# The value product of two attention layers, made by tiles of 128 tokens and brought to the layout by pixel by transfers within SBUF

## What is computed

```python
qkv = (x @ W_qkv).reshape(B, N, P, 3, H, hd)
q = qkv[..., 0, :, :].mean(axis=2).transpose(0, 2, 1, 3)
k = qkv[..., 1, :, :].mean(axis=2).transpose(0, 2, 1, 3)
v = qkv[..., 2, :, :].transpose(0, 3, 1, 4, 2).reshape(B, H, N, hd * P)
scores = jnp.einsum('bhnd,bhmd->bhnm', q, k) * hd ** (-0.5)
attn = jax.nn.softmax(scores, axis=-1)
out = jnp.einsum('bhnm,bhme->bhne', attn, v)
out = out.reshape(B, H, N, hd, P).transpose(0, 2, 4, 1, 3).reshape(B, N, P, C)
return out @ W_proj + b_proj
...
x = x + _L0_conv_ref(_ln_c(x), ...)
t = t + _L0_ffn_ref(_ln_t(t), ...)      # 8 experts, the best 2 for each token
```

## Time and profile before

| | |
|---|---|
| Runs | 572.95, 572.11, 576.06 us |
| Profiled execution | 571.98 us, span 570.2 us |
| TensorE (PE) busy | 528.8 us, 93% of the span |
| ScalarE (ACT) busy | 346.2 us, 61% |
| VectorE (DVE) busy | 339.1 us, 59% |
| GpSimd (POOL) busy | 254.0 us, 45% |
| Mean granted clock of TensorE | 0.98 of full speed |
| Value products L1342 | 5.2% of the chain that ended last |

### The profile page before, as it was taken

The page is one execution under the profiler, slowest core; times in us unless marked ns, Lnnn a source line. Parts: engine busy times, 40 slices in busy tenths (PEclk is TensorE's granted clock), DMA queues, the critical chain, the costliest instruction groups (busy, mean ns, idle before and its releaser), DMA issues.

```text
span 570.2 us, 15336 instructions
## 1 busy us (share of the span) xinstructions
PE 528.8 (93%) x3521; PEld 469.5 (82%) x3522; DVE 339.1 (59%) x791; ACT 346.2 (61%) x676; POOL 254.0 (45%) x278
## 2 busy tenths in 40 slices
PE   8899968999999999999879999699999999999992
PEld 4887537989999999999768875399999999999981
DVE  5548974455533555554794578745667676767441
ACT  4778525666645666666457755555777576766530
POOL 4638222444544454453435360424444445645422
PEclk9999979999999999999989999899999999999997
DMA  8436745786432454125442238364365555312110
GB/s 270 150 111 166 255 128 158 241 214 155 114 74 42 145 119 93 35 37 156 136 151 71 84 103 272 117 219 92 88 190 133 138 142 155 59 30 46 32 19 10
DMA packets 49037, 70.54 MB, mean 124 GB/s; under 512 B 9182, under 2 KB 40560, under 8 KB 49008
## 3 DMA queue, kind: packets, MB, share of 16 engines
q1 hardware_dynamic: 35216, 56.41, 31.4%
q0 software_dynamic: 10464, 13.58, 13.3%
q10 hardware_dynamic: 3328, 0.20, 0.4%
HBM read 57.55 MB, written 13.47 MB: 125 GB/s over the span
## 4 chain that ended last, share of the span: by engine, by line
PE 69%; DVE 10%; DMA 7%; ACT 5%; issue 5%; DVEq 2%; ACTq 1%; POOL 1%; POOLq 0%; SPq 0%
PE banks L1301 16%; PE banks L1303 15%; PE banks L1302 15%; PE banks L1514 6%; PE banks L1342 5%; PE banks L1416 2%; DVE stats L907 2%; PE banks L1479 2%; DMA expert_io<-xn_dram,gcol 2%; DMA out_dram<-region_b,scol 1%; DMA mid_dram<-region_b,scol 1%; PE banks L1353 1%; PE banks L1309 1%; ACT region_a L702 1%; ACT onehot_blk L803 1%
## 5 line engine op out<-in xcount | busy, mean ns | idle before, releaser
L1301 PE MATMUL banks<-w_hi,xT_hi 128*128 x336 | 119.4, 355 | 4.0 <-DVE xT_lo L1173 2.6
L1303 PE MATMUL banks<-w_hi,xT_lo 128*128 x336 | 115.0, 342 | 0.0
L1302 PE MATMUL banks<-w_lo,xT_hi 128*128 x336 | 114.2, 340 | 0.0
L1301 PE MATMUL banks<-w_hi,hT_hi 128*128 x364 | 107.9, 296 | 3.9 <-DVE hT_lo L1248 3.9
L1303 PE MATMUL banks<-w_hi,hT_lo 128*128 x364 | 102.8, 283 | 0.0
L1302 PE MATMUL banks<-w_lo,hT_hi 128*128 x364 | 102.8, 282 | 0.0
L638 POOL DMA_INDIRECT mid_dram<-region_b,scol x26 | 49.5, 1905 | 76.4 <-DMA mid_dram<-region_b,scol 28.4
L611 POOL TENSOR_TENSOR w_lo<-raw,w_hi 128x1024 fp32r<-128x1024 f32 (+2 forms) x24 | 58.9, 2471 | 53.2 <-ACT w_hi L686 43.5
L827 ACT COPY banks<-seed_rows 128x672 f32 (+1 forms) x84 | 69.0, 822 | 20.5 <-DVE h_sb L1265 10.7
L638 POOL DMA_INDIRECT out_dram<-region_b,scol x26 | 45.7, 1759 | 71.3 <-DMA expert_io<-xn_dram,gcol 20.3
L1301 PEld LDWEIGHTS banks<-w_hi,hT_hi 128*128 128x128 f32 x364 | 69.3, 190 | 7.0 <-issue 6.3
(11 more groups left out here) (206 smaller groups left out, 899.2 us busy)
## 6 DMA issues: line engine op xcount, KB each, us to landing
raw<-in_L_ffn_w_dram SPq DMA_DIRECT2D x32, 512.0 KB, 3.7
raw<-in_L_ffn_W_dram SPq DMA_DIRECT2D x16, 672.0 KB, 4.1
seed_rows<-in_L_ffn_b_dram SPq DMA_DIRECT2D x8, 672.0 KB, 4.2
seed_rows<-in_L_ffn_b_dram SPq DMA_DIRECT2D x8, 512.0 KB, 4.0
xn_dram<-raw SPq DMA_DIRECT2D x6, 512.0 KB, 3.1
raw<-in_L_ffn_W_dram SPq DMA_DIRECT2D x8, 384.0 KB, 4.1
raw<-in_L_ffn_W_dram SPq DMA_DIRECT2D x8, 256.0 KB
wqkv<-in_L_conv_W_qkv_dram SPq DMA_DIRECT2D x2, 768.0 KB, 5.7
```

Source lines behind the costliest of these rows:

```text
L1301: pe.matmul(out, hi, w_high, start=first, stop=False, skip_group_check=onto)
L1302: pe.matmul(out, hi, w_low, start=False, stop=False, skip_group_check=onto)
L1303: return pe.matmul(out, lo, w_high, start=False, stop=last, skip_group_check=onto)
```

## The change

**Values by tiles.** `values` now makes one of 12 products of 128 tokens by 264 columns per layer, from consecutive columns of `xnT`, into the bank that `V_BANKS[L]` names. ScalarE copies each into one of three free places (`v_parts`: tiles 0 to 4 in `region_d`, 5 to 9 in the third slot of `w_lo`, 10 and 11 in `region_a`). SP then copies the 256 channels of each tile within SBUF, 128 partitions x 1 KB to 8 partitions x 16 KB of `v_sb` (`values_by_pixel`), and the attention product waits for all of them (`v_early`, `v_late`).

**Logits.** They now come out by token. Three small VectorE products `x_part_of` take them from the copies; the way through DRAM is gone, with its two transfers, `v_logits` and L1048.

**Order.** Products, copies and casts are put in another order, in each layer its own. In layer 1 the column sums stand ahead of layer 0's last expert rows, the centring at the start of VectorE's layer 1, tiles 0 and 1 of the values between the transposes, and ScalarE copies the first two transposes and normalises tile 4 before the last deviations. New waits: GpSimd's piece 8 for `x_part_of(1)`; ScalarE's first attention copy for the first five transfers; ScalarE's cast behind the attention copies for all; SP's load of experts 1 and 2 in layer 0, and of expert 2 in layer 1, stand behind transfers in its list.

```diff
...
+V_BANKS = ((6, 7, 4) * 4, (5, 6, 5, 6, 2, 3, 6, 7, 4, 6, 7, 4))
+V_EARLY = 5
...
+        v_parts = [(slice(0, V_EARLY), region_d[:, 0:V_EARLY * (C + E)]),
+                   (slice(V_EARLY, 2 * V_EARLY), w_lo[:, SLOTS - 1, 0:V_EARLY * (C + E)].bitcast(F32)),
+                   (slice(2 * V_EARLY, TILES), region_a[:, TILES * C:TILES * C + (TILES - 2 * V_EARLY) * (C + E)])]
...
+            def values_by_pixel(L, first, end):
+                for i in range(first, end):
+                    sp.wait_ge(lay[L].v, i + 1)
+                    sp.dma_start(v_sb[NPT * i:NPT * (i + 1), :, :], v_tile(i)[:, 0:C]
+                                 ).then_inc(v_early if i < V_EARLY else v_late, 16)
...
+                    if L == 1 and e == 2:
+                        sp.wait_ge(rows_mm, 6)
+                    if e >= 1:
+                        values_by_pixel(L, *((0, V_EARLY, TILES), (0, 0, TILES))[L][e - 1:e + 1])
...
+                    if q == PIECES * (SLOTS - 1):
+                        pool.wait_ge(x_early, 3 * L + 2)
...
-                deviations(0, 0)
-                normalise(0)
-                deviations(1, 0)
-                deviations(2, 0)
-                normalise(1)
...
-                def values_out(j):
-                    if L == 1 and j == 0:
-                        act.wait_ge(lay[0].store, 96)
-                    for q in (2 * j, 2 * j + 1):
-                        act.wait_ge(s.v_mm, q + 1)
-                        nc.scalar.copy(v_sb[:, q, :], bank[V_BANKS[q % 3]][0:BN, 0:C + E]).then_inc(s.v, 1)
+                def values_out(*tiles):
+                    for i in tiles:
+                        act.wait_ge(s.v_mm, i + 1)
+                        nc.scalar.copy(v_tile(i), bank[V_BANKS[L][i]][:, 0:C + E]).then_inc(s.v, 1)
...
+                deviations(0, 0)
+                normalise(range(0, 4))
+                deviations(1, 0)
+                if L == 0:
+                    deviations(2, 0)
+                    normalise(range(4, 8))
+                    transposed(0)
+                    transposed(1)
+                else:
+                    transposed(0)
+                    transposed(1)
+                    normalise(range(4, 5))
+                    deviations(2, 0)
+                    normalise(range(5, 8))
+                    values_out(0, 1)
+                for j in range(2, 6):
+                    transposed(j)
...
+                    if g == 0:
+                        act.wait_ge(x_early, 3 * L + 1)
+                        act.wait_ge(v_early, 16 * V_EARLY * (L + 1))
...
-                values_out(0)
-                first_high(*((1, 2), (4, 5))[L])
-                values_out(1)
-                first_high(*((2, 3), (5, 6))[L])
-                values_out(2)
-                first_high(*((3, 4), (6, 7))[L])
+                    values_out(0, 1)
+                    first_high(1, 2)
+                    values_out(2, 3, 4)
+                    first_high(2, 4)
+                else:
+                    values_out(2, 3)
+                    first_high(4, 5)
+                    values_out(4, 5)
+                    first_high(5, 6)
+                    values_out(6, 7)
+                    first_high(6, 7)
...
                 exponentials(1)
-                values_out(3)
-                first_high(*((4, 5), (7, 8))[L])
+                values_out(*((5, 6, 7), (8,))[L])
+                if L == 1:
+                    first_high(7, 8)
...
-                values_out(4)
+                values_out(*((8,), (9,))[L])
...
-                values_out(5)
+                values_out(*((9, 10, 11), (10, 11))[L])
...
-                    first_high(5, 6)
-                values_out(6)
+                    first_high(4, 6)
...
-                values_out(7)
-                act.wait_ge(fold, FOLD * (L + 1))
-                act.dma_start(x_logits_dram.rearrange("(n q) e -> n q e", q=PIX), v_logits[:, :, :]
-                              ).then_inc(scores_dma, 16)
+                act.wait_ge(v_late, 16 * (TILES - V_EARLY) * (L + 1))
                 first_high(*((6, 8), (8, 9))[L])
...
+                        act.wait_ge(x_early, 3 * (L + 1))
...
-                act.wait_ge(scores_dma, 16 * (2 * L + 1))
-                act.dma_start(x_logits[:, :, :], x_logits_dram.rearrange("(i p) e -> p i e", p=P)
-                              ).then_inc(scores_dma, 16)
...
+                    centre()
...
+                def x_part_of(n):
+                    tiles, part = v_parts[n]
+                    dve.wait_ge(s.v, min(tiles.stop, TILES))
+                    return nc.vector.tensor_tensor(x_logits[:, tiles, :], part[:, :, C:C + E],
+                                                   std[:, tiles].unsqueeze(2).to_broadcast([P, tiles.stop - tiles.start, E]),
+                                                   ALU.mult)
+
+                dve.wait_ge(s.std, 3)
+                x_part_of(0).then_inc(x_early, 1)
...
-                dve.wait_ge(s.v, PIX)
-                nc.vector.tensor_copy(v_logits[:, :, :], v_sb[:, :, C:C + E]).then_inc(fold, 1)
+                x_part_of(1).then_inc(x_early, 1)
+                x_part_of(2).then_inc(x_early, 1)
...
-                dve.wait_ge(scores_dma, 32 * (L + 1))
+                dve.wait_ge(x_early, 3 * (L + 1))
...
-                chain(nc.vector.tensor_tensor(x_logits[:, :, :], x_logits[:, :, :], tiles_bc(std[:, :]), ALU.mult))
...
+                if L == 0:
+                    column_sums(s.route_in, 48)
...
+                def values(*tiles):
+                    for i in tiles:
+                        if i == 0:
+                            pe.wait_ge(s.conv_in, 48)
+                            pe.wait_ge(fold, FOLD * L + 1)
+                        pe.wait_ge(s.xnT, i // 2 + 1)
+                        here, used = V_BANKS[L][i], V_BANKS[L][0:i]
+                        if here in used:
+                            pe.wait_ge(s.v, max(n for n in range(i) if used[n] == here) + 1)
+                        elif here in XT_BANKS:
+                            pe.wait_ge(s.xm, XT_BANKS.index(here) + 1)
+                        for k in range(KC):
+                            mm = pe.matmul(bank[here][:, 0:C + E], xnT[:, k, i * P:(i + 1) * P],
+                                           wqkv[:, k, 2 * C:3 * C + E], start=(k == 0), stop=(k == KC - 1))
+                        mm.then_inc(s.v_mm, 1)
...
-                def values(j):
-                    for q in (2 * j, 2 * j + 1):
-                        if q == 1:
-                            pe.wait_ge(s.xm, 3)
-                        if q >= 3:
-                            pe.wait_ge(s.v, q - 2)
-                        for k in range(KC):
-                            of_pixel = xnT[:, k, :].rearrange("p (n q) -> p q n", q=PIX)[:, q, :]
-                            mm = pe.matmul(bank[V_BANKS[q % 3]][0:BN, 0:C + E], of_pixel,
-                                           wqkv[:, k, 2 * C:3 * C + E], start=(k == 0), stop=(k == KC - 1))
-                        mm.then_inc(s.v_mm, 1)
+                    if L == 1 and j == 1:
+                        values(0, 1)
...
+                    if g in V_BANKS[L]:
+                        pe.wait_ge(s.v, V_BANKS[L].index(g) + 1)
...
-                pe.wait_ge(s.xnT, 6)
-                pe.wait_ge(s.conv_in, 48)
-                pe.wait_ge(fold, FOLD * L + 1)
-                values(0)
+                if L == 0:
+                    values(0, 1)
+                else:
+                    values(2, 3, 4, 5)
...
+                if L == 1:
+                    pe.wait_ge(s.v, 3)
...
-                values(1)
-                values(2)
+                values(*((2, 3, 4), (6, 7))[L])
...
-                values(3)
+                values(*((5, 6, 7), (8,))[L])
...
-                values(4)
-                values(5)
+                values(*((8, 9, 10, 11), (9, 10, 11))[L])
...
-                values(6)
...
-                values(7)
...
-                pe.wait_ge(s.v, PIX)
...
+                pe.wait_ge(v_early, 16 * V_EARLY * (L + 1))
+                pe.wait_ge(v_late, 16 * (TILES - V_EARLY) * (L + 1))
...
+                    column_sums(lay[1].route_in, 32)
...
```

56 lines of the change are left out of this document (31 added, 25 removed).

## The result

The changed kernel took 594.8 us (median of four runs, 593.31 to 597.13), the kernel before beside it 573.17 (572.11 to 576.06): a ratio of 1.037, 95% interval 1.032 to 1.043. The prediction of 566.8 us and its range of 564.5 to 570.0 were wrong, and wrong in sign. The profiled execution has a span of 592.2 us (before 570.2), so 22.0 us have to be found.

The account below looks back on a forecast made before the run. TensorE was taken to bound the attention stages. Layer 1's -5.8 us and layer 0's +0.3 gave -5.5, from 571.98 to 566.5; adjusted to a median, 566.8 us, range 564.5 to 570.

Parts of the forecast that it names:

- Price of a transfer: Copies of value tiles within SBUF: each lands in 3.5 us, 0.4 us to issue; 4.4 by the port rule.
- slower than before: Both layers: landings over 8 us; at x, layer 1 saves 5.8 - (x - 3.5), layer 0 costs 0.3 + (x - 7.0); chance 0.05.
- Layer 0, TensorE: Layer 0: query/key product at 18.8, transposes end at 37.0, attention product at 38.6, 3.4 us earlier.
- Layer 0 keeps no gain: Layer 0: splits, loads and casts delay the output copies; projection at 53.5 instead of 52.98, costing 0.3 us.
- a GpSimd that is not held: Rival for layer 0: GpSimd works beside the bias sums, projection at 52, 1.6 us more gained, 565.2 us; chance 0.17.
- End of layer 0: Layer 0's last expert rows: column sums delay layer 1's statistics by 0.37 us; VectorE's 0.5 us centring is hidden.
- Layer 1, the hole and the transposes: Before query/key: value tiles 0 and 1 (1.8 us) fill TensorE's 2.25 us idle; twelve transposes take 1.4 to 1.5, not 2.82.
- Layer 1, up to the attention product: Layer 1: query/key at 300.8, last transfer lands and attention product starts at 318.2 instead of 324.04, saving 5.8 us.
- the clock falls in the new wait: Rival for layer 1: 2.8 us idle lowers TensorE's clock, attention products lose about 1.4 us, 568.2 us; chance 0.18.
- The sum: Whole kernel: layer 1's -5.8 us and layer 0's +0.3 us give -5.5 us.

Follow-up runs that it names:

- e2: Changed kernel with each tile's transfer going to 8 partitions 12 apart, the score products reading the keys in that order: 1.014 of the kernel before.
- e1: Changed kernel with the 12 transfers of each layer left out, output not the reference's: 567.88 us, 0.987 of the kernel before.
- e9: e6 with ScalarE's casts of weight pieces 4 and 5 put ahead of its first two attention copies in layer 0: 0.995 of the kernel before.
- e11: e9 with ten filler products ahead of the attention product in both layers, instead of seven in layer 1 only: 0.995 of the kernel before.
- e12: e6 with ten filler products ahead of both layers' attention products and layer 0's first VectorE bias sum moved earlier: 567.49 us, 0.986 of the kernel before.
- e3: Changed kernel with each transfer writing its 128 rows to 128 partitions, output not the reference's: span 569.0 us, one run.
- e6: e5 with, in layer 1, seven filler products ahead of the attention product and b_route moved back behind the normalised tiles: 0.990 of the kernel before.
- e5: e2 with the key order made in VectorE's copy of kT and in the mask, so TensorE reads neighbouring words: 0.993 of the kernel before.
- e13: Changed kernel with the odd tiles' transfers issued by ScalarE on its own DMA queue, the even ones by SP: 588.8 us, one run.

## Why the prediction was wrong, step by step

- **Price of a transfer** (3.5 us to landing, a latency): the step that failed. No trace shows one such transfer alone, but 12 in layer 1 take from the first issue at 314.1 to 341.05, 26.9 us, 2.24 each, so 3.5 for one was not too low. The prediction also has an estimate by the Trainium skill, page "SBUF - State Buffer", section "Door 1: The DMA port swizzle": 2.4 us for the bytes; the trace agrees, with 2.24. The error is that each was given its own 3.5 us as if they ran side by side, and that only the 0.4 us of issue were summed (an issue took 0.61). 12 x 2.24 = 26.9 us do not fit between the first tile at 18.6 and the wanted start at 38.6 (20 us), and the weights of expert 1 are issued in the middle of them. One multiplication would have shown it: the estimate was read as a latency, not as the time for which a transfer occupies the queue.
- **The rival "slower than before"** (chance 0.05, landings of over 8 us because transfers and loads share the queue) named the direction. Its threshold of 8 us is passed in layer 0 with 19 us and just reached in layer 1 (last issue at 332.9, product at 341.05). Put into its own formula these two give some 583 us, not 594.8; most of the rest is the half clock in both products and the late query/key product of layer 1, below. Its reason was only partly right: in layer 1 no load is on its way for 19.5 us and the rate is still 68 GB/s, and e2 keeps all loads and is quick. "The loads were never above 4.7" spoke of loads that are spread over all 128 partitions, so it was no evidence for these transfers. The range had to reach to this case once the estimate of 2.4 us stood beside a count of 12.
- **Layer 0, TensorE**: right. 18.73 for the query/key product (18.8), 37.30 for the end of the transposes (37.0); without transfers the attention product starts at 37.43.
- **Layer 0 keeps no gain**: right, 53.40 in e1 where 53.5 was forecast, and by the path that was forecast: two splits take 5.91 us, 1.2 over 2 x 2.36 (1.6 were forecast), then a load of 3.54, a cast and the output copies. What the prediction left out is the other direction: beside the splits the three bias sums take 5.65 us in e1, and 7.80 in e9, where they are what the product waits for (53.73; 56.46 in e11, with the half clock behind the wait). With neither held up and the clock kept, e12, the projection starts at 51.97, near the 52 that the prediction gave for a GpSimd that is not held.
- **End of layer 0**: the 0.4 us of the column sums are there (0.36 in the chain), but "the centring is hidden in the wait" failed: it started with a GpSimd split and ended with it, 1.7 us on the chain, 4.8 us for the pair in e3. With b_route moved, query/key stands at 19.7, 0.3 before the forecast's 20.5 - 0.5.
- **Layer 1, the hole and the transposes**: right. Tiles 0 and 1 stand in the hole, of which 1.19 us are left, and the twelve transposes take 1.53 us instead of 2.82.
- **Layer 1, up to the attention product**: with quick transfers right: from query/key to the attention product 17.6 us in e6 (17.4 forecast). In the changed kernel it is 22.3.
- **The rival "the clock falls in the new wait"** (0.18): it happened, and not only behind the long wait: the product of layer 1 took 10.36 us in the changed kernel (7.36 us idle ahead of it), 10.48 in e3 (1.50 idle), 9.75 in e5 (2.63 idle), and 7.3 in e1 (no idle) and e6 (filler); in layer 0 of the changed kernel the granted clock is 0.50, the level of 1.2 GHz, in the row at 55.00 above. It cost 2.6 us in layer 0 (9.79 against 7.16) and 3.2 in layer 1 (10.36 against 7.15), not the 1.4 forecast: in layer 1 the granted clock is 0.50 from 341.0 on and 1.00 only from 348 on.
- **The sum**: -5.5 was forecast. e12, with quick transfers, b_route and the sum moved and filler that was in no forecast, is at 0.986 of before, some 8 us, interval 5 to 11. It is another kernel than the one forecast, so it does not bear out the -5.5.

## What to carry to other kernels

For several transfers in a row, add up what each occupies (bytes over the rate that its narrower side allows) and set the sum against the time in which they must all be through; a time to landing is the price of the last one only. Look at which partitions a transfer writes: here a permutation of the destination, taken up for nothing in the order of the keys, took the ratio to the kernel before from 1.037 to 0.993. And before putting a small VectorE operation beside GpSimd's elementwise work, look at what queues behind it: it may end only when GpSimd's instruction does.

## What the runs showed of the hardware

- 8 destination partitions with a step of 1, 2, 4 and 12: 55 to 68, 118, 191 and 187 GB/s, at the same 0.52 to 0.57 share of the DMA engines. Slow transfers hold the engines busy and slow the loads that follow on the queue (512 KB: 8.8 us to landing, 4.6 in the same kernel without the transfers).
- Two queues do not run two such transfers side by side for long (e13: the product of layer 0 starts 5.3 us earlier, that of layer 1 no earlier). The Trainium skill, page "SBUF - State Buffer", section "Can I just issue two DMAs to hit both halves?", says of two at once, to partitions 0 and 64, that they serialise, measured there at +6%; the trace, for other partitions, agrees in layer 1 (71 GB/s; 68 with one queue) and shows up to 111 GB/s in a stretch of layer 0.
- Some VectorE operations and GpSimd's splits exclude each other for a whole instruction: a product over 8 elements in each partition took 2.42 us in the changed kernel, 0.23 without a split beside it, and two in a row 4.83 in e3. Not all do: an operation with a PSUM operand beside the same splits took 0.18 (L968). The Trainium skill, page "SBUF - State Buffer", section "SBUF: two separate sides", tells of an exclusive lock on a shared pair of ports, held for the whole instruction; the trace agrees for the operations that were held, also for ones this small.
- A matmul whose moving operand has a step of 8 words took 0.354 us instead of 0.248 (96 columns, f32), and the mask product 0.857 instead of 0.358 (384 columns, bf16).
